# Streams of constant products on TensorE in the waits of a macaron transformer block

## The chip, the cores and the metric

The kernel runs on one core of one Trainium2 chip. The time is that of the device in microseconds (us): one launch, the median of three runs. The engines are PE (TensorE, matrix products; PEld is its weight load), DVE (VectorE), ACT (ScalarE), POOL (GpSimd) and SP (SyncE, which here issues most DMAs). PE's clock has two levels, 2.4 GHz and 1.2 GHz; the profile shows the granted one as 1.00 and 0.50, and a mean in between where a stretch has both.

## The reference

Three layers in a row over 2048 tokens of width 128, everything in f32. Cut to what matters:

```python
x = x + 0.5 * ffn(layernorm(x))          # layer 0
x = x + attention(layernorm(x))          # layer 1: 16 heads of 8, causal, 2048 keys
x = x + 0.5 * ffn(layernorm(x))          # layer 2, as layer 0

def ffn(x):                              # itself attention and then a mixture of experts
    h = rmsnorm(x, ln1_w)
    x = x + softmax(causal(rope(h @ wq) @ rope(h @ wk).T / sqrt(8))) @ (h @ wv) @ wo
    h = rmsnorm(x, ln2_w)
    probs = softmax(h @ router_w)                        # 8 experts
    topv, topi = top_k(probs, 2); topv /= topv.sum()
    weights = one_hot(topi) @ topv
    moe = sum over experts of (silu(h @ w_gate[e]) * (h @ w_up[e]) * weights[e]) @ w_down[e]
    return x + moe
```

Every expert has 448 hidden units. Only the two experts chosen for a token are computed.

## The kernel before

One loop `Fori(0, 3)` runs over the layers; layers 0 and 2 take the router and expert blocks, layer 1 jumps over them. A layer has three blocks, and at the end of a block each engine drains and all five meet at a barrier.

*Block 1, projections and attention.* The tokens are normalised, turned (L764) and projected in four chunks of 512 (L773 for the four q and k products with 512 columns, L781 for v). The rotated q and k are split into three bf16 parts, written to DRAM and read back as operands `qa` and `ka` of 96 rows. Behind the projections PE waits on `terms_ready` and `values_ready`, and then, for the first attention product (L809), on those loads. Attention has 16 chunks (4 head groups by 4 query chunks) and two streams of work on PE: "fillers" in banks 4 to 6, above all the row maxima (L809 and mask L812, reduced by DVE at L598), and the main stream, scores (L855, banks 0 to 3), exponentials on ACT (L747), weighted values (L868, bank 7). The order of both is computed ahead by `core_schedule()`, a list of events with estimated times; the change does not touch it. At the end of a chunk ACT copies the output (L754), PE turns it (L823, event "normalise") and DVE divides (L623, L624). When a query chunk is done in the last head group, PE turns it once more (L832, "turn"), DVE adds the bias (L632), and PE projects it (L840, "project"); DVE adds the residual and sums squares (L638 to L658). The last query chunk does this with nothing else left to do on PE.

*Block 2, the router.* DVE makes 16 normed tiles (L932), PE turns them (L885) and multiplies them with the router's 8 columns (L890, 16 f32 products of 8 columns, two records each in a trace). A chain of small DVE operations (L943 to L960) chooses the two experts per token. PE counts with two products (L896, L897); a second chain on DVE (L968 to L1026) makes the places of the tokens in expert slots and the one-hot tiles `moves` and `places`; PE multiplies these in 32 f32 products of 78 columns (L902), whose result DVE turns into the row numbers for the gathers (L1031 to L1034).

*Block 3, the experts.* POOL gathers 39 slots of 128 tokens by indirect DMA (L1053); PE turns a slot (L1103), multiplies with gate and up weights (L1118), turns the activation (L1127) and multiplies with the down weights (L1136). ACT and DVE work in between.

Bank 0 is written in block 1 by the first turns and by scores, in block 3 by the gate products; between these nobody reads it. `ones` is a 128 by 128 f32 tile of ones made once at the start and used as the left factor of L897.

Of the kernel before, what the change touches and what calls it, by code (L numbers as in the profile page):

```python
# [17 lines left out]
NC = T // CH  # L18
# [147 lines left out]
def macaron_kernel(nc, x_in, w5, b4, vecs, wo_w, rope, router, w_gate, w_up, w_down, out):  # L166
# [48 lines left out]
    ones = sb("ones", [128, 128])  # L215
# [132 lines left out]
    chunks, events, _ = core_schedule()  # L348
# [39 lines left out]
    def key_guard(b):  # L388

        return ka[64:96, b, :, :].rearrange("p h t -> p (h t)").bitcast(F32)  # L390


    with nc.Block() as block:

# [65 lines left out]
    with nc.Fori(0, NLAYER) as layer:  # L460

        with nc.Block() as block:
# [294 lines left out]
            def _(pe):  # L757
# [26 lines left out]

                pe.wait_ge(terms_ready, 4 * NC)
                pe.wait_ge(values_ready, NC)
                mi = 0
                pe.wait_ge(wo_loaded, 16)  # L790
                for ev in events:
# [6 lines left out]
                    if kind == "rowmax":  # L798
                        _, j, qt, h0, some, kc, final = ev
                        g, c = chunks[j]  # L800
                        b = g % 2
                        if qt == 0 and h0 == 0 and (kc == 0 or c == 0):
                            pe.wait_ge(group_loaded[g] if g else chunk_loaded[c], 16 * 6)
                        tile = TPC * c + qt
                        n = min(CH, (tile + 1) * 128 - kc * CH)
                        diag = kc == c
                        for k in range(some):
                            dst = ps[:, bank, k * n:(k + 1) * n]
                            ins = pe.matmul(dst, qa[0:KROWS, b, h0 + k, tile * 128:(tile + 1) * 128],  # L809
                                            ka[0:KROWS, b, h0 + k, kc * CH:kc * CH + n], start=True, stop=not diag)  # L810
                            if diag:
                                ins = pe.matmul(dst[:, n - 128:n], identb[:, :], mask_rows[:, :],  # L812
                                                start=False, stop=True)
                        ins.then_inc(filler_ready, 1)
                    elif kind == "maxout":
                        j = ev[1]
                        pe.wait_ge(maxima_ready, j + 1)
                        pe.transpose(ps[0:16, bank, 0:128], mx[:, j % MD, :], identf[:, :]).then_inc(filler_ready, 1)
                    elif kind == "normalise":
                        j = ev[1]  # L820
                        pe.wait_ge(output_copied, j + 1)
                        for k in range(TPC):
                            ins = pe.transpose(ps[:, bank, k * 128:(k + 1) * 128],  # L823
                                               otf[:, j % 2, k * 128:(k + 1) * 128], identf[:, :])
                        ins.then_inc(filler_ready, 1)
                        written = mi
                    elif kind == "turn":

                        c = ev[1]
                        pe.wait_ge(filler_used, written)  # L830
                        for k in range(TPC):
                            ins = pe.transpose(ps[:, bank, k * 128:(k + 1) * 128], onat[:, TPC * c + k, :], identf[:, :])  # L832
                        ins.then_inc(filler_ready, 1)
                        written = mi
                    elif kind == "project":
                        c = ev[1]
                        pe.wait_ge(filler_used, written)
                        for k in range(TPC):
                            t = TPC * c + k
                            ins = pe.matmul(ps[:, bank, k * 128:(k + 1) * 128], hT[:, t * 128:(t + 1) * 128],  # L840
                                            wos[:, 0:D], start=True, stop=True)
                        ins.then_inc(filler_ready, 1)
                    elif kind == "scores":
                        _, s, j, kt, h = ev
                        g, c = chunks[j]
                        b = g % 2
                        if kt == 0 and h == 0:
                            pe.wait_ge(guard_ready[j % MD], 16 * (j // MD + 1))
                        q0 = max(0, kt - TPC * c) * 128
                        n = CH - q0  # L850
                        u = HPG * s + h
                        if u >= SB:
                            pe.wait_ge(probs_ready, u - SB + 1)
                        dst = ps[:, u % SB, 0:n]
                        pe.matmul(dst, ka[0:KROWS, b, h, kt * 128:(kt + 1) * 128],  # L855
                                  qa[0:KROWS, b, h, c * CH + q0:(c + 1) * CH],
                                  start=True, stop=True).then_inc(scores_ready, 1)
                    elif kind == "values":
                        _, s, j, kt = ev
                        g, c = chunks[j]  # L860
                        q0 = max(0, kt - TPC * c) * 128
                        pe.wait_ge(probs_ready, HPG * (s + 1))
                        if kt >= TPC * c:
                            pe.wait_ge(masked, masks_to(j, kt))
                        if kt == 0 and j >= 1:
                            pe.wait_ge(output_copied, j)
                        for h in range(HPG):
                            ins = pe.matmul(ps[32 * h:32 * h + HD + 1, SB + MB, q0:CH],  # L868
                                            vv[:, kt, g * HPG + h, :], probs[:, s % 2, h, 0:CH - q0],
                                            start=kt == 0, stop=kt == TPC * (c + 1) - 1)  # L870
                        ins.then_inc(values_weighted, 1)


        with nc.Block() as block:

            @block.tensor
            def _(pe):
                with pe.If(layer != 1):
                    for c in range(NC):
                        if c >= 2:  # L880
                            pe.wait_ge(h2_copied, c - 1)
# [9 lines left out]
                                        start=True, stop=True)  # L891
                    ins.then_inc(logits_ready, 1)

                    pe.wait_ge(taken_ready, 1)
                    taken = gw[:, 5, :, :].rearrange("p t e -> p (t e)")
                    pe.matmul(ps[:, 7, 0:TT * E], below[:, :], taken, start=True, stop=True)  # L896
                    pe.matmul(ps[:, 7, TT * E:2 * TT * E], ones[:, :], taken, start=True, stop=True).then_inc(ranks_ready, 1)  # L897
                    pe.wait_ge(moves_ready, 1)
                    for q in range(NK // 8):
                        pe.wait_ge(places_ready, q + 1)  # L900
                        for k in range(8 * q, 8 * q + 8):
                            ins = pe.matmul(ps[:, 4, 0:2 * NSLOT], places[:, k, :],  # L902
                                            moves[:, k, :, :].rearrange("p s u -> p (s u)"),
                                            start=k == 0, stop=k == NK - 1)
                    ins.then_inc(slots_ready, 1)

            @block.scalar
            def _(act):
# [135 lines left out]
        with nc.Block() as block:  # L1044
# [53 lines left out]
            def _(pe):  # L1098
# [4 lines left out]
                    pe.transpose(ps[:, 7, 0:128], xring[:, u % XR, :], identf[:, :]).then_inc(tile_turned, 1)  # L1103

                with pe.If(layer != 1):
                    turn(0)
                    experts = []
                    for i in range(NSLOT + 2):
# [175 lines left out]
```

## Time and profile before

| | us |
|---|---|
| median of three runs | 1919.13 |
| lowest and highest run | 1913.59, 1921.05 |
| the profiled execution | 1916.23 |
| its span, first to last instruction | 1914.7 |
| PE busy | 1698.2 (89%) |
| DVE busy | 1369.8 (72%) |
| ACT busy | 1073.3 (56%) |
| mean granted clock of PE | 0.91 |

Times in the profile count from the start of the span. Layer 0 goes from there to about 709 us, layer 1 to 1221 us. A row of the timeline gives the start, the duration of the merged group, the engine, the line, what it writes and reads, its size and its count, and in brackets the idle time of the engine before it with what ended it. A busy PE is not PE at its peak: the same product at half the clock is busy for about twice the time. A record of PE includes the time until its last column is out, so products in a row are better priced from start to start.

### The profile page before, as it was taken

The page shows a single profiled execution, that of the slowest core. Times are in us where ns is not written, and L with a number is a line of the kernel's source. Part 1 is how long each engine was busy: PE and PEld are TensorE (multiplying, and loading weights), DVE is VectorE, ACT ScalarE, POOL GpSimd, SP SyncE. Part 2 cuts the span into 40 slices and gives each one's busy share as a digit, 9 for nine tenths or more (in the row PEclk, how much of TensorE's full clock was granted, in tenths as well). Part 3 has the DMA queues.
Part 4 walks back from the last instruction along what each step waited for, and adds up shares of the span by engine and source line. Part 5 has one row for each costly group of instructions (what it writes and reads, how often), then busy time and mean ns, then how long its engine had stood idle before and what let it go on. Part 6 is the DMA issues. An engine that isn't in the chain of part 4 may idle for free. (4 is left out here: it accounts for less than half of the span.)

```text
span 1914.7 us, 30151 instructions
## 1 busy us (share of the span) xinstructions
PE 1698.2 (89%) x10630; PEld 740.2 (39%) x10630; DVE 1369.8 (72%) x2705; ACT 1073.3 (56%) x2301; POOL 445.3 (23%) x491
## 2 busy tenths in 40 slices
PE   4899999999749947899999999579999999984895
PEld 2333333333247733233333342233333333324674
DVE  8788998986253338888999983388889998815333
ACT  3355777677604423356777678235576767771442
POOL 6300201111015647000102020260010100110564
PEclk9688999999859977889999999778899999995898
DMA  4500203300011135200202000242010020000113
GB/s 131 128 7 3 51 2 106 63 2 2 8 29 39 44 93 150 51 1 2 51 2 51 2 2 2 66 138 44 2 35 19 2 51 2 2 8 22 37 42 87
DMA packets 59432, 75.61 MB, mean 39 GB/s; under 512 B 9527, under 2 KB 52092, under 8 KB 57976
## 3 DMA queue, kind: packets, MB, share of 16 engines
q1 hardware_dynamic: 50056, 62.10, 12.6%
q0 software_dynamic: 4992, 9.32, 1.8%
q10 hardware_dynamic: 4224, 2.10, 0.4%
q8 instruction: 95, 1.56, 0.4%
q14 instruction: 65, 0.53, 0.1%
HBM read 52.97 MB, written 21.43 MB: 39 GB/s over the span
## 5 line engine op out<-in xcount | busy, mean ns | idle before, releaser
L747 ACT ACTIVATE probs<-ps 128x512 f32<-128x512 f32 (+3 forms) x1920 | 879.0, 543 | 471.7 <-PE ps L855 470.3
L598 DVE TENSOR_REDUCE mpart<-ps 128x1 f32<-128x512 f32 (+3 forms) x1680 | 1014.6, 665 | 115.9 <-PE ps L809 65.1
L809 PE MATMUL ps<-ka,qa 96*128 96x512 bf16 (+3 forms) x1920 | 670.3, 371 | 36.3 <-DMA ka<-ksplit 22.8
L855 PE MATMUL ps<-qa,ka 96*128 96x512 bf16 (+3 forms) x1920 | 617.0, 357 | 1.1 <-DMA qa<-guard 0.5
L868 PE MATMUL ps<-probs,vv 128*9 128x512 f32 (+3 forms) x3840 | 442.5, 533 | 8.8 <-ACT probs L747 8.1
L696 POOL TENSOR_SCALAR_AFFINE_SELECT probs<-probs 128x512 f32<-128x512 f32 x192 | 121.8, 634 | 1178.5 <-ACT probs L747 1178.5
L809 PEld LDWEIGHTS ps<-ka,qa 96*128 96x128 bf16 x1920 | 191.9, 101 | 480.2 <-DVE mpart L598 339.1
L855 PEld LDWEIGHTS ps<-qa,ka 96*128 96x128 bf16 x1920 | 183.7, 100 | 187.1 <-ACT probs L747 69.1
L812 PE MATMUL ps<-mask_rows,identb 128*128 128x128 bf16 x768 | 162.0, 236 | 0.0
L1189 DVE SCALAR_TENSOR_TENSOR probs<-probs,slot_w,ps 128x448 f32<-128x448 f32 x78 | 53.0, 680 | 120.0 <-PE ps L1118 120.0
L868 PEld LDWEIGHTS ps<-probs,vv 128*9 128x9 f32 x3840 | 57.8, 88 | 158.3 <-ACT probs L747 116.3
L1053 POOL DMA_INDIRECT arena<-tokens,from_row x78 | 76.8, 984 | 136.3 <-issue 79.8
L1063 POOL DMA_INDIRECT results<-hT,to_row x78 | 78.5, 1007 | 74.2 <-issue 42.1
L623 DVE RECIPROCAL rden<-ps 128x16 f32<-128x16 f32 x48 | 12.0, 250 | 113.3 <-PE ps L823 113.0
L812 PEld LDWEIGHTS ps<-mask_rows,identb 128*128 128x128 bf16 x768 | 80.4, 105 | 28.9 <-issue 2.2
L1136 PE MATMUL ps<-wds,probs 112*128 x624 | 82.8, 276 | 1.4 <-DVE hT L1196 1.2
L1147 ACT ACTIVATE hT<-ps 128x128 f32<-128x128 f32 x78 | 21.6, 277 | 110.3 <-PE ps L1103 110.3
L1136 PEld LDWEIGHTS ps<-wds,probs 112*128 112x128 f32 x624 | 75.8, 192 | 2.3 <-issue 2.3
L1118 PE MATMUL ps<-wgs,hT 128*128 x156 | 74.8, 562 | 0.8 <-ACT hT L1147 0.5
L1164 ACT ACTIVATE probs<-ps 112x512 f32<-112x512 f32 x78 | 46.6, 597 | 51.1 <-PE ps L1127 51.1
L1118 PE MATMUL ps<-wus,hT 128*128 x156 | 73.6, 555 | 0.0
L1158 ACT ACTIVATE probs<-ps 128x448 f32<-128x448 f32 x78 | 42.4, 543 | 39.4 <-PE ps L1118 39.2
(163 smaller groups left out, 1070.6 us busy)
## 6 DMA issues: line engine op xcount, KB each, us to landing
qa<-qsplit SPq DMA_DIRECT2D x27, 384.0 KB
ka<-ksplit SPq DMA_DIRECT2D x27, 384.0 KB
probs<-rope SPq DMA_DIRECT2D x12, 512.0 KB, 6.8
qa<-qsplit SPq DMA_DIRECT2D x36, 96.0 KB
ka<-ksplit SPq DMA_DIRECT2D x36, 96.0 KB
qsplit<-arena SPq DMA_DIRECT2D x6, 384.0 KB, 3.2
ksplit<-arena SPq DMA_DIRECT2D x6, 384.0 KB, 2.8
tokens<-arena SPq DMA_DIRECT2D x2, 1024.0 KB, 5.1
```

The lines of the kernel that those rows point to most:

```text
L598: dve.tensor_reduce(mpart[:, j % MD, h0:h0 + some, qt, kc], ps[:, bank, 0:some * w].rearrange("p (h w) -> p h w", h=some), axis=AX.X, op=A ...
L696: pool.affine_select(out=own, in_=own, compare_op=ALU.is_ge, fill=0.0, base=0, pattern=[[0, HPG], [1, 128]], channel_multiplier=-1).then_i ...
L747: act.activation(probs[:, s % 2, h, 0:n], ps[:, u % SB, 0:n], ACT.Exp, scale=SCALE).then_inc(probs_ready, 1)
L809: ins = pe.matmul(dst, qa[0:KROWS, b, h0 + k, tile * 128:(tile + 1) * 128], ka[0:KROWS, b, h0 + k, kc * CH:kc * CH + n], start=True, stop= ...
L812: ins = pe.matmul(dst[:, n - 128:n], identb[:, :], mask_rows[:, :], start=False, stop=True)
L855: pe.matmul(dst, ka[0:KROWS, b, h, kt * 128:(kt + 1) * 128], qa[0:KROWS, b, h, c * CH + q0:(c + 1) * CH], start=True, stop=True).then_inc( ...
L868: ins = pe.matmul(ps[32 * h:32 * h + HD + 1, SB + MB, q0:CH], vv[:, kt, g * HPG + h, :], probs[:, s % 2, h, 0:CH - q0], start=kt == 0, sto ...
L1053: pool.indirect_dma_start(xring[:, u % XR, :], None, tokens, bass.IndirectOffsetOnAxis(ap=from_row[:, u:u + 1], axis=0)).then_inc(tile_loa ...
L1063: pool.indirect_dma_start(results, bass.IndirectOffsetOnAxis(ap=to_row[:, u:u + 1], axis=0), obuf[:, u % OR, :], None, bounds_check=TOPK * ...
L1118: pe.matmul(ps[:, 2 * (i % 2) + k, 0:M], xt[:, i % 2, :], w[:, bass.ds(expert, 1), :].rearrange("p o m -> p (o m)"), start=True, stop=True ...
L1136: ins = pe.matmul(ps[:, 6, 0:D], atb[u % 2][:, k, :], wds[0:MR, bass.ds(experts[u], 1), k, :].rearrange("p o d -> p (o d)"), start=k == 0, ...
L1189: dve.scalar_tensor_tensor(acb[i % 2], sgb[i % 2], slot_w[:, i:i + 1], ps[:, 2 * (i % 2) + 1, 0:M], ALU.mult, ALU.mult).then_inc(act_ready, 1)
```

## The change

`spin(pe, n)` issues products of `ones` with itself, repeated over up to 512 columns, into bank 0: n is the number of 128-column pieces. Nobody reads the result and nothing waits for a semaphore of it, but PE works in order, so what stands behind a stream begins when the stream is through, and a block's end waits for it. Streams are added at eleven places; those of 26, 11 and the three of 2 run in all layers, the others in layers 0 and 2.

```diff
+    def spin(pe, n):
+        wide = ones[:, :].rearrange("p (o c) -> p o c", o=1)
+        for k in range(0, n, 4):
+            m = min(4, n - k)
+            pe.matmul(ps[:, 0, 0:m * 128].rearrange("p (o c) -> p o c", o=m), ones[:, :],
+                      wide.broadcast_to([128, m, 128]), start=True, stop=True)
...
+                spin(pe, 26)
                 pe.wait_ge(terms_ready, 4 * NC)
                 pe.wait_ge(values_ready, NC)
...
                     elif kind == "normalise":
                         j = ev[1]
+                        if j == len(chunks) - 1:
+                            spin(pe, 2)
                         pe.wait_ge(output_copied, j + 1)
...
                     elif kind == "turn":
                         c = ev[1]
+                        if c == NC - 1:
+                            spin(pe, 2)
                         pe.wait_ge(filler_used, written)
...
                     elif kind == "project":
                         c = ev[1]
+                        if c == NC - 1:
+                            spin(pe, 2)
                         pe.wait_ge(filler_used, written)
...
                         ins.then_inc(values_weighted, 1)
+                spin(pe, 11)
...
                 with pe.If(layer != 1):
+                    spin(pe, 8)
                     for c in range(NC):
...
                     ins.then_inc(logits_ready, 1)
+                    spin(pe, 22)
                     pe.wait_ge(taken_ready, 1)
...
                     pe.matmul(ps[:, 7, TT * E:2 * TT * E], ones[:, :], taken, start=True, stop=True).then_inc(ranks_ready, 1)
+                    spin(pe, 52)
                     pe.wait_ge(moves_ready, 1)
...
                     ins.then_inc(slots_ready, 1)
+                    spin(pe, 4)
...
                 with pe.If(layer != 1):
+                    spin(pe, 14)
                     turn(0)
```

From the end of attention to the first expert product, PE's program reads before, in the order in which PE takes it (the sizes are rows by columns of the output; the branches between the blocks are left out):

```order
L868 MATMUL ps<-probs,vv 9x128 x4
L823 MATMUL ps<-identf,otf 128x128 x4
L832 MATMUL ps<-identf,onat 128x128 x4
L840 MATMUL ps<-wos,hT 128x128 x4
...
L885 MATMUL ps<-identf,arena 128x128 x16
L890 MATMUL ps<-rts,hT 128x8 x16
L896 MATMUL ps<-rec,below 128x128
L897 MATMUL ps<-rec,ones 128x128
L902 MATMUL ps<-arena,probs 128x78 x32
...
L1103 MATMUL ps<-identf,arena 128x128 x2
```

Each of these rows from L823 on has a wait ahead of it, L890 and L897 excepted. In the changed kernel, whose own line numbers stand here, PE's program at the tail of attention reads (L833, L844 and L854 are L823, L832 and L840 of before):

```order
L882 MATMUL ps<-probs,vv 9x128 x4
L397 MATMUL ps<-ones 128x256
L833 MATMUL ps<-identf,otf 128x128 x4
L397 MATMUL ps<-ones 128x256
L844 MATMUL ps<-identf,onat 128x128 x4
L397 MATMUL ps<-ones 128x256
L854 MATMUL ps<-wos,hT 128x128 x4
L397 MATMUL ps<-ones 128x512 x2
L397 MATMUL ps<-ones 128x384
```

Three short streams stand ahead of the three waits, and the one of 11 closes the block. PE's program through the router and up to the first slot of the experts reads (L901 and L906 are L885 and L890 of before, L913, L914 and L920 are L896, L897 and L902):

```order
L397 MATMUL ps<-ones 128x512 x2
L901 MATMUL ps<-identf,arena 128x128 x16
L906 MATMUL ps<-rts,hT 128x8 x16
L397 MATMUL ps<-ones 128x512 x5
L397 MATMUL ps<-ones 128x256
L913 MATMUL ps<-rec,below 128x128
L914 MATMUL ps<-rec,ones 128x128
L397 MATMUL ps<-ones 128x512 x13
L920 MATMUL ps<-arena,probs 128x78 x32
L397 MATMUL ps<-ones 128x512
...
L397 MATMUL ps<-ones 128x512 x3
L397 MATMUL ps<-ones 128x256
```

Nothing changes places: the L397 rows are added between the old ones, ahead of the instruction that waits.

## Rows read from the trace of the kernel before

**Rows 1.** The page: parts 1 (busy, share) and 2 (PE's clock in 40 slices).

```profile
PE 1698.2 (89%) x10630; PEld 740.2 (39%) x10630; DVE 1369.8 (72%) x2705; ACT 1073.3 (56%) x2301; POOL 445.3 (23%) x491
...
PEclk9688999999859977889999999778899999995898
```

**Rows 2.** Waits of PE: us in total, times, longest.

```profile
PE ps L809 <- DMA ka<-ksplit: 22.8, 3, 7.8
```

**Rows 3.** Stretches: length, busy us (instructions) by engine, PE's clock, DMA share, GB/s.

```profile
45.00:49.00 4.00, 0.00 (x0) 0.00 (x0) 3.64 (x3) 2.44 (x5) 3.82 (x4) 0.53 0.79 205
49.00:55.00 6.00, 5.08 (x29) 2.92 (x30) 3.93 (x8) 1.74 (x2) 5.35 (x7) 0.50 0.81 243
...
58.00:69.00 11.00, 9.51 (x34) 3.71 (x33) 9.47 (x18) 2.52 (x5) 6.49 (x9) 0.54 0.46 115
...
168.00:512.00 344.00, 339.73 (x2357) 121.96 (x2355) 272.11 (x519) 250.62 (x550) 43.49 (x55) 1.00 0.13 32
```

**Rows 4.** Timeline, DVE: start, us, engine, line, what, [idle before, releaser].

```profile
51.07 6.13 DVE L598 TENSOR_REDUCE mpart<-ps 128x4 f32<-128x512 f32 x11 [2.28 <-PE ps L812]
...
517.20 0.69 DVE L638 TENSOR_TENSOR rec<-ps,vbc 128x512 f32<-128x512 f32 x1 [2.23 <-PE ps L840]
...
519.81 0.08 DVE L658 DVE_READ_ACCUMULATOR2_ANT rst<- 128x1 f32 x1
...
537.92 0.29 DVE L968 COPY rec<-ps 128x128 f32<-128x128 f32 x1 [0.64 <-PE ps L897]
```

**Rows 5.** Timeline, PE, L832 and L840 of two chunks.

```profile
481.71 0.66 PE L832 MATMUL ps<-identf,onat 128*128 128x128 f32 x4
...
484.14 1.16 PE L840 MATMUL ps<-wos,hT 128*128 128x128 f32 x8
...
513.09 1.09 PE L832 MATMUL ps<-identf,onat 128*128 128x128 f32 x4 [0.83 <-DVE onat L624]
...
515.12 2.05 PE L840 MATMUL ps<-wos,hT 128*128 128x128 f32 x8 [0.93 <-DVE hT L632]
```

**Rows 6.** Timeline, PE, the router and the first experts of layer 0.

```profile
522.68 4.27 PE L885 MATMUL ps<-identf,arena 128*128 128x128 f32 x16 [5.52 <-DVE arena L932]
526.79 4.00 PE L890 MATMUL ps<-rts,hT 128*128 128x8 f32 x32
536.66 0.79 PE L896 MATMUL ps<-rec,below 128*128 128x128 f32 x2 [5.87 <-DVE rec L960]
...
550.84 13.94 PE L902 MATMUL ps<-arena,probs 128*128 128x78 f32 x64 [12.96 <-DVE arena L1026]
570.18 0.47 PE L1103 MATMUL ps<-identf,arena 128*128 128x128 f32 x1 [5.41 <-DMA arena<-tokens,from_row]
...
572.35 1.86 PE L1118 MATMUL ps<-wgs,hT 128*128 x2 [0.49 <-ACT hT L1147]
```

**Rows 7.** Stretches of the tail, the router and the first experts.

```profile
508.00:512.00 4.00, 2.42 (x32) 0.96 (x24) 0.00 (x0) 2.12 (x8) 1.27 (x2) 1.00 0.00 0
...
526.00:529.00 3.00, 3.00 (x26) 2.82 (x25) 0.57 (x3) 2.48 (x3) 0.00 (x0) 0.92 0.47 136
...
528.00:530.00 2.00, 2.00 (x19) 2.00 (x19) 0.00 (x0) 0.89 (x1) 0.00 (x0) 0.98 1.01 289
...
552.00:564.00 12.00, 12.00 (x58) 12.00 (x57) 2.19 (x2) 0.00 (x0) 0.00 (x0) 0.50 0.00 0
...
576.00:578.00 2.00, 2.00 (x4) 0.86 (x4) 0.50 (x1) 0.77 (x2) 0.04 (x1) 0.58 0.13 33
```

**Rows 8.** Timeline, PE, products in a row during the projections.

```profile
26.72 1.06 PE L781 MATMUL ps<-otf,hT 128*128 128x128 f32 x8
27.66 3.70 PE L773 MATMUL ps<-hT,otf 128*128 128x512 f32 x8
31.20 0.60 PE L764 MATMUL ps<-identf,onat 128*128 128x128 f32 x4
```

**Rows 9.** Timeline, PE, the first wait for row maxima.

```profile
57.56 0.27 PE L818 MATMUL ps<-identf,mx 128*16 128x128 f32 x1 [1.63 <-DVE mx L605]
```

## The prediction

> **What bounds the kernel now.** I read the page's first two parts, then the granted clock in stretches, then PE's waits, then PE's timeline at the places where products are added. The reader is to see first that PE is busy 1698.2 us (89% of the span) and that its clock is not at full height everywhere: the line PEclk is at 10 tenths in the middle of each layer and at 5 to 8 at its edges [rows 1]. PE's clock has two levels here, 1.00 (2.4 GHz) and 0.50 (1.2 GHz). Between 168 and 512 us it stays at 1.00 with PE busy 339.7 of 344 us; there the change adds nothing [rows 3]. So the change can only win where PE works at 0.50 and something waits for it, and can only lose where a stream outlasts the wait in which it stands. Around PE's long waits I see four such places.
>
> 1. The start of attention. PE waits 7.8 us for ka [rows 2], the clock falls to 0.53 in that wait, and 49 to 55 us run at 0.50 [rows 3]. But VectorE reduces the row maxima there in one piece, 11 reductions in 6.13 us from 51.07 us on [rows 4]: it is the slower one, and PE waits for it right behind.
> 2. The tail of attention. L832 and L840 of the last chunk take 1.09 and 2.05 us at the low clock where the same lines took 0.66 and 1.16 us for another chunk at 481 to 485 us [rows 5].
> 3. The router (layers 0 and 2). DVE works a long chain of small operations; PE waits 5.87 us for `taken` and 12.96 us for `moves`, and then makes the 32 products of L902 (78 columns, two records each) in 13.94 us, all at 0.50, while DVE waits [rows 6, 7].
> 4. The first experts: from 572.35 us PE works without a gap, at 0.50 and, around 577 us, 0.58 [rows 6, 7]. From there to the end of the layer PE is what everybody waits for.
>
> **The price of a stream.** One f32 product of 512 columns: L773 begins at 27.66 and the line behind four of them at 31.20 us, 0.885 us each, or 0.221 us for 128 columns at 1.00 [rows 8]. At 0.50 the four L840 products of 128 columns take 2.05 us with their end [rows 5], so about 0.43 us for 128. The streams are then, high or low: 26 units 5.75 or 11.2 us; 2 units 0.44 or 0.9; 11: 2.4 or 4.7; 8: 1.8 or 3.4; 22: 4.9 or 9.5; 52: 11.5 or 22.4; 4: 0.9 or 1.7; 14: 3.1 or 6.0. What raises the clock shows at L885: 16 transposes begin at 522.68 us at 0.50, and at 526 to 529 us it is 0.92 [rows 6, 7]. A dense stream should do the same in a few us.
>
> The Trainium skill ("TensorE: Matmul & The Clock Gate", Part 4: PE-mode transpose) says that the full clock does not engage for PE's transposes. This trace disagrees, by those two rows: only transposes stand between 522.68 us and the rise. By the page L890 behind them would be slow before and after alike, and the term of L890 below would be nothing, 3.8 us less in the whole sum.
>
> **The change, part by part.** Of one router layer:
> - *Tail.* The streams of 2 stand in waits of 0.8 to 0.93 us [rows 5] and hide at either clock within 0.1 us. If they hold the clock, L832 and L840 return to 0.66 and 1.16 us: -1.3 us. If not, 0. I take -1.3, since the stretch before, 508 to 512 us, holds 1.00 with PE busy only 2.42 of 4 us [rows 7], and the streams only add to that.
> - *Streams of 11 and 8.* The 11 run beside DVE's last residual work: L840's consumer starts at 517.20 us and the last small operation of the block at 519.81 [rows 4], a cover of 2.6 us against 2.4 (or 4.7 at the low clock: up to +1.6). The 8 stand in the wait of L885 (5.52 us in all with what lies before). I take 0.
> - *L890.* A hazard that the change makes itself. Before, the clock rises just as L890 begins and falls at its end. Weight loads take 2.00/19 = 0.105 us at 0.98 and 12.00/57 = 0.21 us at 0.50 [rows 7], and L890 is 32 of them. After the change PE comes in at the high clock, the transposes (one per 0.27 us, half as dense as at low) and then 8-column products follow, and the clock should fall in L890 instead of rising before it. Ends 0 and +3.4; I take +1.9.
> - *Stream of 22.* It starts at the end of L890, then probably at 0.50, and rises on the way: 5 to 8 us against a wait of 5.87; L896 and L897 behind it fall from 1.26 us (536.66 to DVE's L968 at 537.92) to about 0.7 (4 records of 0.117 and their end) [rows 4, 6]. Ends -0.6 and +2.0; I take +0.7.
> - *Stream of 52.* 11.5 us at 1.00 in a wait of 12.96: hidden, 1.5 us of idleness left. (At 0.50 all through: +9.4, a rival below.)
> - *L902.* At the high clock the nearest row is L781, 8 records of 128 columns in 0.94 us from start to start [rows 8]: 64 x 0.117 = 7.5 us against 13.94. Ends 0 and -6.4. The remaining 1.5 us gap is the trouble: a wait of 1.63 us at 57 us was followed by 0.54 from 58 on [rows 3, 9]. L902 has more loading than streaming, and never got the clock up in 14 us. I take -4.0: the clock held for about two thirds of it.
> - *Stream of 4* lies beside the four small DVE operations that end the block; 0 or, low, +0.9: +0.3.
> - *Stream of 14 and first experts.* It stands in the 4 us between the block's start and the first gathered tile (570.18 us). All at 1.00, the 5.35 us from 572.35 shrink by half, -2.7; if it outlasts the tile, +0.9 comes back. I take -2.1.
>
> Sum of a router layer: -1.3 + 1.9 + 0.7 - 4.0 + 0.3 - 2.1 = -4.5 us, twice: -9.0. Layer 1 has the tail alone: -1.3 (DVE ends its block there too). The start of attention, three times: the stream of 26 is hidden (5.75 of 7.8 us, at 1.00 since the projections before it are), but DVE is behind PE; what is won is the first group of four, 0.85 us at low and half at high: -0.4, with ends +1.7 and -2 for cold stretches that move later in the layer. Three: -1.2. In all -11.5 us (-9.0, -1.3, -1.2). Against the execution's own 1916.23 us (span 1914.7 and 1.5 around it) this is 1904.7. The median of the three runs, 1919.13, stands 2.9 above that execution, so the forecast is 1907 to 1908; I say **1907**.
>
> **Rivals.**
> *A. Short gaps leave the clock alone.* L890 keeps its speed, L902 runs all at 1.00, the experts too: per router layer -1.3 - 0.6 - 6.4 - 2.7 = -11.0; with layer 1 and better starts -25 us: 1894. For it: 504 to 512 us stays at 1.00 in spite of waits of 0.8 us. Against: the fall behind 57 us. The Trainium skill (same page, "Why this matters for your kernels") has this rule, that only idle gaps longer than those left here throttle the engine; this trace speaks against it with the same fall.
> *B. The clock falls in the rest of the wait before L902.* The sum without the 4.0: -0.5 per router layer, -1.3, -1.2, in all -3.5 us: 1915.6. For it: L890 and L902 at 0.50 all through and the 57 us case. Against: only 1.5 of 13 us remain idle.
> *C. The streams run low and outlast their waits.* The point from which it decides is the clock at the end of L890. If the stream of 22 needs the whole low time (9.5 against 5.9 us, +3.6), a third of the 52 runs low too (7.7 and 7.5 against 12.96, +2.2), L890 takes its +3.4, and neither L902 nor the experts gain: +9.2 per router layer, 1919.1 + 18.4 = 1937.5. If constants do not raise the clock at all, the 52 alone add 9.4, beyond that. Against it: projections, transposes and experts each raised the clock while they ran. That is also the case in which the change doesn't do what it says.
>
> **How the numbers follow.** Forecast 0.42, A 0.15, B 0.35, C 0.08. The range: A's end (1894) to a little above B (1915.6 and what DVE-bound starts may cost), 1893 to 1920; C is left out. What can be told from no change is 0.5%, 9.6 us: below 1909.5 is faster. Faster: A and three quarters of the forecast's own spread, 0.49. Within 0.5%: B and the rest, 0.43. Slower: C, 0.08.
>
> **What would show it.** The clock in the stretch of L902 and its duration: 7.5 us (A), 9 to 11 (forecast), 13.9 (B). L890: 4.0 us or 5 to 7. L896's idle time: none if the 22 outlast the wait. L1118's first pair: 1.86 or 0.92 us. L840 at the tail: 1.16 or 2.05. PE's wait for `moves` is to shrink from 12.96 to about 1.5 us; if instead DVE's row L968 starts later relative to L943 than 7.1 us, the stream of 22 costs more than I said. The forecast is wrong if L902 gains nothing, or if attention in any layer, from its first L855 to its last L823, moves by more than 2 us.

## The result, and the profile after

| | before | after |
|---|---|---|
| median, run side by side (20 runs each) | 1917.32 | 1913.14 |
| lowest and highest run | 1913.59, 1923.58 | 1909.39, 1917.88 |
| the profiled execution | 1916.23 | 1914.05 |
| its span | 1914.7 | 1912.5 |
| mean granted clock of PE | 0.910 | 0.938 |

The ratio of the times is 0.9975, with a 95% interval of 0.9967 to 0.9982. The kernel became 4.2 us faster, where the prediction summed 11.5 us. It is a real gain, smaller than the 0.5% that the prediction took as its bound, and inside its range; but the size is off by a factor of 2.7, and one term of the sum carries most of that.

The page of the kernel after, parts 1 and 2 (busy time; PE's clock in 40 slices), answers to [rows 1]:

```profile
PE 1767.2 (92%) x10812; PEld 764.4 (40%) x10812; DVE 1370.8 (72%) x2705; ACT 1073.0 (56%) x2301; POOL 445.0 (23%) x491
...
PEclk9789999999979978889999999887999999998998
```

PE is busy 69 us longer and has 182 more instructions, all of them streams, and the clock is higher in the slices at the ends of attention. DVE has as much to do as before.

PE's timeline of layer 0 from the tail of attention to the first experts (start, us, engine, line, what, and in brackets the idle time before it with its releaser). L833, L844, L854 are L823, L832, L840 of before; L901, L906, L913, L914, L920 are L885, L890, L896, L897, L902; L1122 and L1138 are L1103 and L1118. It answers to [rows 5, 6]:

```profile
515.10 0.66 PE L844 MATMUL ps<-identf,onat 128*128 128x128 f32 x4 [0.31 <-DVE onat L631]
515.59 0.60 PE L397 MATMUL ps<-ones 128*128 128x256 f32 x2
516.59 1.16 PE L854 MATMUL ps<-wos,hT 128*128 128x128 f32 x8 [0.41 <-DVE hT L639]
517.59 2.53 PE L397 MATMUL ps<-ones 128*128 128x512 f32 x6
521.18 1.98 PE L397 MATMUL ps<-ones 128*128 128x512 f32 x4 [1.07 <-PEq L469]
523.27 4.27 PE L901 MATMUL ps<-identf,arena 128*128 128x128 f32 x16
527.38 5.60 PE L906 MATMUL ps<-rts,hT 128*128 128x8 f32 x32
532.84 8.02 PE L397 MATMUL ps<-ones 128*128 128x512 f32 x12
540.69 0.38 PE L913 MATMUL ps<-rec,below 128*128 128x128 f32 x2
540.91 0.39 PE L914 MATMUL ps<-rec,ones 128*128 128x128 f32 x2
541.14 11.32 PE L397 MATMUL ps<-ones 128*128 128x512 f32 x26
554.26 12.34 PE L920 MATMUL ps<-arena,probs 128*128 128x78 f32 x64 [1.80 <-DVE arena L1045]
566.40 2.00 PE L397 MATMUL ps<-ones 128*128 128x512 f32 x2
568.86 5.37 PE L397 MATMUL ps<-ones 128*128 128x512 f32 x8 [0.47 <-PEq L889]
574.06 0.27 PE L1122 MATMUL ps<-identf,arena 128*128 128x128 f32 x1
...
575.78 1.01 PE L1138 MATMUL ps<-wgs,hT 128*128 x2 [0.69 <-ACT hT L1167]
```

And the stretches of the kernel after (length, busy us by PE, PEld, DVE, ACT, POOL, then the clock, DMA share, GB/s), to set beside [rows 7]:

```profile
523.00:527.00 4.00, 3.84 (x16) 1.98 (x15) 4.00 (x16) 1.66 (x3) 0.00 (x0) 1.00 0.00 0
528.00:533.00 5.00, 5.00 (x29) 5.00 (x29) 0.00 (x0) 1.46 (x2) 0.00 (x0) 0.57 0.75 212
541.00:552.00 11.00, 11.00 (x29) 4.90 (x27) 9.87 (x32) 0.00 (x0) 0.00 (x0) 1.00 0.00 1
554.00:556.00 2.00, 1.74 (x15) 1.74 (x16) 2.00 (x3) 0.00 (x0) 0.00 (x0) 1.00 0.00 0
556.00:566.00 10.00, 10.00 (x50) 10.00 (x49) 1.62 (x2) 0.00 (x0) 0.00 (x0) 0.50 0.00 0
569.00:573.00 4.00, 4.00 (x5) 1.69 (x6) 2.27 (x4) 0.00 (x0) 2.91 (x3) 0.50 0.06 16
576.00:578.00 2.00, 2.00 (x7) 1.02 (x7) 0.33 (x1) 1.52 (x3) 1.39 (x3) 1.00 0.20 39
```

Read the two together. The tail is short again. The transposes now run at 1.00, and behind them the clock falls inside L906 (0.57), so the stream of 22 starts low: 8.02 us, where 22 x 0.221 would be 4.9. The stream of 52 stands at 1.00 all through, but 1.80 us are left behind it. L920 starts high and is low from 556 us on, 1.8 us behind its start (1.3 us in layer 2): some 15 of its 64 records lie in the 2 us at 1.00, and the rest in the 10 us at 0.50. It hands a low clock to the streams of 4 and 14, and that of 14 (5.37 us) holds back the first slot. Only then is the clock up.

Segments between the starts of instructions, in us (of a router layer, layer 0 and layer 2; the names are those of before):

| from, to | before | after | predicted change |
|---|---|---|---|
| last L823, last L840 (also layer 1) | 4.75, 4.75 | 3.40, 3.40 | -1.3 |
| last L840, first L885 | 5.94, 5.94 | 5.80, 5.80 | 0 |
| L890, L943 | 4.04, 4.03 | 5.64, 4.44 | +1.9 |
| L943, L968 | 7.09, 7.09 | 8.32, 7.87 | +0.7 |
| L902, L1031 | 13.98, 13.98 | 12.38, 12.78 | **-4.0** |
| L1031, first L1103 | 5.37, 4.61 | 7.42, 7.00 | +0.3, with the row below -1.8 in all |
| first L1103, last L1136 | 120.71, 121.28 | 117.64, 117.51 | |
| last L823, last L1136 | 178.91, 178.72 | 177.62, 175.82 | -4.5 |

### The profile page after: what moved, and what is told of

Same layout as the page of the kernel before. It is cut to its first block and busy times, and to the rows that moved or that the text cites. A ratio compares the mean times of both kernels' runs of the same rounds, so it can differ in the third digit from the quotient of the medians.

```text
span 1912.5 us, 30506 instructions
## 1 busy us (share of the span) xinstructions
PE 1767.2 (92%) x10812; PEld 764.4 (40%) x10812; DVE 1370.8 (72%) x2705; ACT 1073.0 (56%) x2301; POOL 445.0 (23%) x491
## 5 line engine op out<-in xcount | busy, mean ns | idle before, releaser
L820 PE MATMUL ps<-mask_rows,identb 128*128 128x128 bf16 x768 | 157.8, 231 | 0.0
L1209 DVE SCALAR_TENSOR_TENSOR probs<-probs,slot_w,ps 128x448 f32<-128x448 f32 x78 | 53.1, 680 | 115.9 <-PE ps L1138 115.9
L397 PE MATMUL ps<-ones 128*128 128x512 f32 (+2 forms) x182 | 87.0, 624 | 3.1 <-PEq L469 2.1
L1138 PE MATMUL ps<-wgs,hT 128*128 x156 | 71.6, 541 | 1.2 <-ACT hT L1167 1.2
L1138 PE MATMUL ps<-wus,hT 128*128 x156 | 71.4, 539 | 0.0
```

The lines of the kernel that those rows point to most:

```text
L397: pe.matmul(ps[:, 0, 0:m * 128].rearrange("p (o c) -> p o c", o=m), ones[:, :], wide.broadcast_to([128, m, 128]), start=True, stop=True)
L1138: pe.matmul(ps[:, 2 * (i % 2) + k, 0:M], xt[:, i % 2, :], w[:, bass.ds(expert, 1), :].rearrange("p o m -> p (o m)"), start=True, stop=True ...
```

## The experiments

Two theories of the missing gain were on record before them. *The wait* (first theory): the 1.8 us of idleness that the stream of 52 leaves before L902 make the clock fall in it. *Too thin* (second theory): L902, which loads weights longer than it streams, cannot hold the high clock whatever stands before it. For L890's loss the suspicion was the streams of 11 and 8, which bring PE in high so that it falls in L890. Runs e1 to e4 are compared with one set of runs of the kernel before, e5 to e8 with a second, both on one chip on which the kernel before takes 1933.73 and 1935.49 us; e9 to e12 with a third, on another chip where it takes 1919.32. In brackets behind a ratio stands its 95% interval. Lengths of stretches go from the start of one PE or DVE instruction to the start of another.

**e1: the stream of 52 made 58**, six pieces (1.3 us) longer. This and the next diffs are against the changed kernel.

```diff
-                    spin(pe, 52)
+                    spin(pe, 58)
```

> The changed kernel with the stream of 52 made 58, so that it reaches almost up to L920 (L902 of before): the wait of 1.80 us ahead of it should shrink to about 0.5 us. Theory 1 (the wait makes the clock fall): L920 then runs at 1.00, about 7.5 us instead of 12.3 and 12.7, and the kernel gains 9 to 10 us against the changed one, about 1904. Theory 2 (L920 itself is too thin to hold the clock, whatever stands ahead): it starts at 1.00, falls within some 3 to 4 us all the same, lasts 10 to 11 us, and the kernel gains 3 to 4 us.

Measured: 1919.98 us against 1933.73, ratio 0.9924 (0.9911 to 0.9938). L902 to L1031 took 7.41 us in both layers. PE's timeline and a stretch of e1:

```profile
534.34 12.61 PE L397 MATMUL ps<-ones 128*128 128x512 f32 x30
547.46 7.37 PE L920 MATMUL ps<-arena,probs 128*128 128x78 f32 x64 [0.51 <-DVE arena L1045]
```

```profile
547.00:555.00 8.00, 7.54 (x65) 7.45 (x66) 3.95 (x6) 0.00 (x0) 0.00 (x0) 1.00 0.01 2
```

The same 64 records, as thin as before, stay at 1.00 throughout with PEld busy 7.45 of 8 us. *Too thin* falls; *the wait* stands. The price of 7.5 us that the prediction worked out for the high clock [rows 8] was right. The longer stream does two things at once, though: it shortens the wait and adds 1.3 us of dense products ahead of it, and no run separates the two; "the wait" stands for both here. By the ratios e1 is 12 us faster than the changed kernel on the same chip (e5), more than the 9 to 10 us of the first theory: the first slot is no longer held up either (5.34 and 4.64 us from L1031 to L1103, against 7.38 and 7.36 in e5).

**e2: without the streams of 11 and 8.**

```diff
-                spin(pe, 11)
...
-                    spin(pe, 8)
```

> The changed kernel without the streams of 11 and 8. Theory 1 (they bring PE to the router's transposes at the high clock, which then falls in the 8-column products): the transposes begin at 0.50, the clock rises in them or right behind, L906 (L890 of before) lasts 4.0 us again instead of 5.60 and 4.41, and the stream of 22 starts at or near 1.00 and ends before DVE has the sets: 1.0 to 2.8 us less per router layer up to L968, 2 to 4 us in all. Theory 2 (the loss there is chance): L906 lasts as in the changed kernel and the whole is within 1 us of it.

Measured: 1933.63 us, ratio 0.9992 (0.9983 to 1.0001). L890 became slower, not faster: 6.87 us in both layers to DVE's L943. PE's timeline and stretches of e2:

```profile
519.32 4.42 PE L901 MATMUL ps<-identf,arena 128*128 128x128 f32 x16 [5.52 <-DVE arena L951]
523.54 6.84 PE L906 MATMUL ps<-rts,hT 128*128 128x8 f32 x32
```

```profile
519.00:524.00 5.00, 4.68 (x19) 3.46 (x20) 4.21 (x16) 2.01 (x4) 0.00 (x0) 0.50 0.00 0
524.00:530.00 6.00, 6.00 (x29) 6.00 (x30) 0.00 (x0) 1.66 (x2) 0.00 (x0) 0.50 0.62 178
```

The first theory was wrong, and so is the notion that the two streams cause the loss at L890. Without the streams the clock is at 0.50 from the transposes to the end of L890. The same 16 transposes raised it in the kernel before [rows 6, 7] and did not here: with the tail at the high clock and 5.52 us of waiting behind it, the rise before L890 did not come. Every layer of the kernel before, e4 and e12, which all have the tail at the low clock, shows 4.00 to 4.04 us there, and both layers of e2 6.87; why the same transposes raise the clock in the one case and not in the other is open. A sum should not have taken the rise as given.

**e3: without the streams of 4 and 14.**

```diff
-                    spin(pe, 4)
...
-                    spin(pe, 14)
```

> The changed kernel without the streams of 4 and 14. From L1031 (slot weights copied) to the last down product of the layer it took 126.0 us before and 125.1 and 124.5 us after the change. Theory 1 (they win 2.7 us at the first experts and give half of it back by holding up the barrier and the first slot's turn): this kernel is 1 to 1.5 us slower per router layer than the changed one, 2 to 3 in all. Theory 2 (they give back all of it): within 0.5 us.

Measured: 1928.22 us, ratio 0.9960 (0.9945 to 0.9974), better than the whole change (e5 below). L1031 to the first L1103 is 5.34 and 4.69 us again, 2.0 and 2.7 less than with the streams at the low clock, and the experts from L1118 to the last L1136 take 126.33 and 125.00 us against e5's 125.48 and 125.83. Neither theory held: the first had expected e3 to be slower, the second equal. e3 begins its experts at 0.50 and e5 at 1.00, and over the two layers they take the same time: on this chip, where that stretch scatters by over 2 us from kernel to kernel (125.0 to 127.8), a warm start can't be seen.

**e4: the stream of 26 alone**, all others taken out.

> The kernel before with the stream of 26 behind the projections alone, in three layers. My prediction's term: -1.2 us in all, with attention starting at the high clock. Rival: since DVE sets the pace there, the clock falls a few us later instead, the gain is nothing, and the stretch from the first maxima product to the last turn of attention stays 462, 459 and 459 us within the scatter of 1 to 2 us that comes from where the clock happens to fall.

Measured: 1933.90 us, ratio 0.9992 (0.9980 to 1.0004): not to be told from nothing. The other segments came back to those of before: tail 4.75, L890 4.03, L902 to L1031 13.98 in both layers.

**e5: the changed kernel again**, with these.

> The changed kernel again, on the chip of these runs, to compare the others with on one chip. Where the experts take 126 us in every kernel (as in the four runs before, against 116 to 119 us in the two first profiles), its gain at the first experts, 2.7 us per router layer, should be lost and only the cost of the streams of 4 and 14 be left: ratio to the kernel before 0.998 to 1.000 instead of 0.9975.

Measured: 1934.06 us against 1935.49, ratio 0.9988 (0.9977 to 1.0000). Its router is that of the first profile (L902 to L1031 12.41 and 12.44; L1031 to L1103 7.38 and 7.36), with L890 at 5.69 and 5.72. But from L1118 to the last L1136 it takes 125.48 us where the first profile has 115.92 (layer 0). The waits of layer 0 between 600 and 680 us (us in total, times, longest), and that stretch, of e5:

```profile
ACT probs L1184 <- remote: 27.0, 9, 3.2
DVE probs L1209 <- PE ps L1138: 21.8, 13, 2.0
POOL results L1082 <- DVE hT L1216: 18.2, 8, 2.4
DVE hT L1216 <- remote: 17.4, 8, 2.3
```

```profile
600.00:680.00 80.00, 76.07 (x414) 52.52 (x413) 23.32 (x48) 31.76 (x73) 48.28 (x49) 1.00 0.14 39
```

In the first profile of the kernel after, the same stretch reads:

```profile
600.00:680.00 80.00, 80.00 (x463) 58.33 (x463) 26.43 (x55) 38.33 (x82) 53.26 (x54) 1.00 0.17 44
```

On the one chip PE is what everybody waits for (80.00 of 80 us); on the other each engine does about a tenth less in the same 80 us, with waits whose releaser the profile does not show. It was so in every kernel on that chip (experts of 125 to 128 us in all eight, e4 without any stream in the router among them), so it is no effect of the change, and it hides the gain of warm first experts there. What slows that chip is open.

**e6: 58, without 4 and 14.**

```diff
-                    spin(pe, 52)
+                    spin(pe, 58)
...
-                    spin(pe, 4)
...
-                    spin(pe, 14)
```

> 58 in place of 52, and no streams of 4 and 14. Theory (the two parts are independent): it has the 5 us per router layer of the 58 and, where the experts aren't held up by PE, 0.5 to 2 us more per router layer than with the streams of 4 and 14; about 0.989 to 0.992. Rival (L920 leaves the clock high, and the streams of 4 and 14 cost nothing at the high clock, as in the run with 58, where the first slot's turn came 5.34 us behind the copy of the slot weights, as early as before): within 1 us of the run with 58 alone, 0.9924.

Measured: 1926.84 us against 1935.49, ratio 0.9950 (0.9937 to 0.9963), against e1's 0.9924. L902 to L1031 is 7.41 again. Behind a high L902 the streams of 4 and 14 cost nothing (e1: L1031 to L1103 5.34 and 4.64 with them, 5.22 and 4.71 without), and the experts took 127.63 and 127.75 us here against 126.0 in both layers of e1. Neither expectation held: e6 is neither faster than e1 nor within 1 us of it, but 5 us slower by the ratios. A warm start is not the reason, since the first experts begin at 0.50 in both (562.5 to 565.8 us in e1, 565.0 to 568.6 us in e6); 1.6 to 1.7 us per layer lie within the scatter of that stretch on this chip, and what made the rest is open. In e3 the same edit won; in e6 it lost. Up to the first slot the two streams are harmless where the clock is handed to them high, and a delay of 0.7 to 2.7 us where it is low (e2, e5, e7).

**e7: without the three streams of 2.**

> The changed kernel without its three streams of 2 at the tail of attention. Theory (they alone keep the clock up there): last turn to last project product takes 4.75 us again instead of 3.40, in all three layers, 4 us in all, if the rest stays. Rival: the 1.35 us come back in what follows, since L906 (the 8-column products) meets the change of the clock at another moment: L906 back at 4.0 us, and the total within 1 us of the changed kernel.

Measured: 1937.85 us, ratio 1.0005 (0.9994 to 1.0016). PE's timeline of e7:

```profile
517.02 2.04 PE L854 MATMUL ps<-wos,hT 128*128 128x128 f32 x8 [0.94 <-DVE hT L639]
518.85 3.89 PE L397 MATMUL ps<-ones 128*128 128x512 f32 x6
```

The tail is at 4.75 us in all three layers, so the streams of 2 are worth 1.35 us each time. In layers 0 and 2 it also takes 6.67 us instead of 5.80 from L840 to L885: the stream of 11 starts low, needs 3.89 us, and now outlasts DVE's last residual work. That is the hazard which the prediction priced at up to +1.6 and set at nothing; the streams of 2 are what keeps it away. Up to L1031 the parts add up to 3.7 us: 3 x 1.35 + 2 x 0.87 for the lost streams, 2 x 0.6 for a slower L902, less 2 x 1.0 for L890 and 2 x 0.65 for the stream of 22 behind it. From L1031 to the last L1136 e7 takes 1.0 and 0.4 us more than e5. By the ratios e7 stands 3.3 us worse than e5 (0.0017 of 1935); the two intervals, each 4 us wide, overlap, so the segments show this loss and the totals alone do not. The theory held; the rival saw something true, since L890 came back to 4.69 us, but not enough of it.

**e8: 58, without 4 and 14, and the router's turns filled.** A bf16 product of the identity with itself stands behind each of the 16 transposes.

```diff
                             ins = pe.transpose(ps[:, 4 + c % 2, k * 128:(k + 1) * 128], h2[:, t, :], identf[:, :])
+                            pe.matmul(ps[:, 0, 0:128], identb[:, :], identb[:, :], start=True, stop=True)
```

> As the run with 58 and without 4 and 14, and a bf16 product of 128 columns (identity by identity, into bank 0) behind each of the 16 turns of the router. Theory (the thin pace of the turns at the high clock and then of the 8-column products makes the clock fall in them): the clock stays high into the 8-column products, which last 4.0 to 5 us instead of 5.6 to 5.7, and the stream of 22 ends in time: 1 to 2 us less per router layer. Rival (the 8-column products alone let it fall): no change, or up to 1 us more, since each turn has another product ahead.

Measured: 1920.75 us against 1935.49, ratio 0.9922 (0.9907 to 0.9936); e6, which differs by the filling alone, has 0.9950. L890 to L943 falls to 3.73 us, L943 to L968 to 6.97, in both layers. That is more than the 1 to 2 us per router layer that were expected: 3.2 us in these two segments, 2.7 by the ratios. The clock now stays high to the end of L890, so the 8-column products alone do not let it fall; the cause of L890's loss in the changed kernel is the sparse turns at the high clock.

**e9: all streams, 58, the turns filled.**

> All streams of the changed kernel, 58 in place of 52, and a bf16 product behind each of the 16 turns of the router. The runs so far give the parts: L920 7.4 us, the 8-column products 3.7 us, the first experts 1.7 us shorter than without the streams of 4 and 14, at no cost since they run at the high clock. It should be the fastest of all: about 3 us under the run with 58 alone and 3 us under the one that filled the turns without 4 and 14, a ratio of 0.990 to 0.991. Rival: the scatter of where the clock falls in attention (3 us per layer) swallows it.

Measured: 1897.50 us (6 runs, 1893.63 to 1904.34) against 1919.32, ratio 0.9890 (0.9872 to 0.9909). PE's timeline and stretches of e9 (its lines behind the turns are one higher):

```profile
522.72 3.69 PE L907 MATMUL ps<-rts,hT 128*128 128x8 f32 x32
526.26 6.67 PE L397 MATMUL ps<-ones 128*128 128x512 f32 x12
...
546.33 7.37 PE L921 MATMUL ps<-arena,probs 128*128 128x78 f32 x64 [0.50 <-DVE arena L1046]
553.53 1.07 PE L397 MATMUL ps<-ones 128*128 128x512 f32 x2
555.17 3.26 PE L397 MATMUL ps<-ones 128*128 128x512 f32 x8 [0.58 <-PEq L889]
559.08 0.33 PE L1123 MATMUL ps<-identf,arena 128*128 128x128 f32 x1 [0.65 <-DMA arena<-tokens,from_row]
560.37 0.33 PE L1123 MATMUL ps<-identf,arena 128*128 128x128 f32 x1 [0.96 <-DMA arena<-tokens,from_row]
561.34 1.73 PE L1139 MATMUL ps<-wgs,hT 128*128 x2 [0.64 <-ACT hT L1168]
```

```profile
518.00:522.00 4.00, 3.88 (x29) 2.08 (x28) 3.96 (x16) 1.38 (x3) 0.00 (x0) 1.00 0.00 0
522.00:526.00 4.00, 4.00 (x38) 3.78 (x36) 0.44 (x2) 2.29 (x3) 0.00 (x0) 1.00 0.64 181
526.00:533.00 7.00, 7.00 (x19) 3.43 (x19) 5.49 (x21) 0.31 (x1) 0.00 (x0) 0.76 0.17 49
546.00:553.00 7.00, 6.67 (x60) 6.68 (x60) 3.67 (x4) 0.00 (x0) 0.00 (x0) 1.00 0.01 2
561.00:565.00 4.00, 3.67 (x6) 1.84 (x7) 0.31 (x1) 2.03 (x4) 3.05 (x4) 0.57 0.19 49
```

L890 is high to its end; the clock falls only behind it, in the stream of 22 (0.76), where there is slack for it. L902 stays high, the stream of 14 takes 3.26 us and waits for the first slot instead of holding it back (0.65 us for the DMA). But the first experts are not warm: the stream of 14 ends at 558.4 us, PE makes two single turns in the 2.9 us behind it, and the first pair of L1139 (L1118 of before) takes 1.73 us, not 1.01 as in the changed kernel, with the clock at 0.57 from 561 to 565 us. The "1.7 us shorter" first experts of the expectation did not come (125.21 and 124.86 us from L1031 to the last L1136, against 125.39 and 125.15 in e12 below, which has neither stream). This is the best version measured.

**e10: e9 without the stream of 26.**

> The same without the stream of 26 at the start of attention. Theory (it wins nothing, since DVE sets the pace there and the clock falls a little later anyway): the same time within 2 us. Prediction's term: 1.2 us slower. Attention from the first maxima product to the last turn stays 458 to 462 us in each layer either way.

Measured: 1903.67 us, ratio 0.9912 (0.9897 to 0.9928). The medians are 6.2 us apart, more than the 2 us that were expected, but the interval meets that of e9. From the first L809 to the last L823, 33 layers of eleven profiles with the stream of 26 take 460.2 us in the mean and 9 layers of three without it 461.2, with an error of about 0.5 on the difference. In e10 this stretch takes 461.8, 461.9 and 462.2 us, in e9 459.2, 459.1 and 462.1; single layers lie between 457.9 and 463.1 in all fourteen profiles. The term may be -1 us per layer, or nothing.

**e11: 55**, half way between 52 and 58.

> The changed kernel with 55 in place of 52: the wait ahead of L920 becomes about 1.2 us, between the 1.8 us after which the clock fell in L920 and the 0.5 us after which it held. Theory 1 (any short wait will do as long as most of the time around it is dense): L920 takes 7.4 us as with 58, ratio 0.993. Rival: 1.2 us is too long as well, and L920 takes 10 to 12.4 us, at least in one of the two layers.

Measured: 1907.04 us, ratio 0.9927 (0.9905 to 0.9948). PE's timeline of e11:

```profile
538.62 11.97 PE L397 MATMUL ps<-ones 128*128 128x512 f32 x28
551.74 7.37 PE L920 MATMUL ps<-arena,probs 128*128 128x78 f32 x64 [1.15 <-DVE arena L1045]
```

1.15 us of waiting leave the clock high in both layers (L902 to L1031 7.41 and 7.41); 1.80 us did not, in any of the ten router layers that had it (the first profile, e2, e3, e5, e7: 12.4 to 13.0 us). Nothing between 1.15 and 1.80 us was tried.

**e12: the kernel before with the stream of 22 and one of 58 alone.**

> The kernel before with only two streams, 22 and 58, in the router. Theory (the parts are independent): the stream of 22 starts low and delays L968 by up to 1 us, the 58 starts high or nearly so, L920 takes 7.4 us; 5 to 6 us less per router layer, ratio 0.994 to 0.995. Rival: the 58 start partly low, last over 13 us, and L920 starts 1 to 3 us late: ratio 0.996 to 0.998.

Measured: 1906.40 us, ratio 0.9934 (0.9921 to 0.9947). Two streams of eleven places bring more than the whole change does (0.9975) and over half of what e9 does: L902 to L1031 7.41 us in both layers. L890 is at 4.00 and 4.03 as before, and L943 to L968 is 8.32 and 8.29, 1.2 us more than before: the stream of 22 starts low and outlasts DVE's chain. Its first experts begin low too. PE's timeline and a stretch of e12:

```profile
568.23 1.85 PE L1138 MATMUL ps<-wgs,hT 128*128 x2 [0.49 <-ACT hT L1167]
```

```profile
568.00:572.00 4.00, 3.77 (x6) 1.94 (x7) 0.30 (x1) 2.05 (x4) 2.98 (x4) 0.50 0.20 49
```

## Why the prediction was right in its sign and wrong in its size

**The step that failed** is the term "L902: I take -4.0: the clock held for about two thirds of it". It measured -1.6 and -1.2 us; over two layers 5.2 us of the missing 7.3. The prediction had all that it needed: a price of 7.5 us at the high clock, which all seven profiles with a high L902 confirm (7.41), the rest of the wait (1.5 us, in truth 1.8), and a row with a wait of 1.63 us and a fall behind it [rows 3, 9]. It then split the difference between the two ends. No run showed such a middle: either the product stays high (waits of 0.5 and 1.15 us, -6.6 us), or the clock falls 1 to 2 us into it (wait of 1.8 us, -1.0 to -1.6). That is close to rival B, and nearer to it than to the forecast in size: B's sum was -3.5 us, the forecast's -11.5, the runs gave -4.2. B was not exact either, since the clock did not fall in the wait but just behind it. The row that argued for B should have weighed more than the argument that only 1.5 of 13 us remain idle.

**The stream of 22** was given +0.7 and cost +1.2 and +0.8. It starts at 0.50 and takes 8.02 us (7.57 in layer 2) against the 5 to 8 that were named; L896 had no idle time left, as the prediction said it would show. The mechanism was right, the value too small.

**L890** was given +1.9 and cost +1.6 and +0.4 (+1.7 in e5). The size was about right, the cause only half. The clock does fall inside it when PE comes in high behind the transposes, as the prediction said; but e2 shows that it is worse when PE comes in low behind a high tail (6.87 us): the rise that the prediction read from [rows 6, 7] is not to be had from 16 transposes in every case. What decides is that the clock is high when L890 begins and that the turns before it are dense enough to keep it so (e8, e9: 3.73).

**The end of the router and the first experts** were given -1.8 in all (streams of 4 and 14, first experts) and brought -1.0 and -1.4 (126.08 and 125.88 us from L1031 to the last L1136 before, 125.06 and 124.51 after). The first pair of L1118 took 1.01 us, high as predicted. The stream of 14 was costed at the high clock with +0.9 for a miss; handed the low clock by L902 it took 5.37 us and delayed the first slot by 2.0 and 2.4 us, which warm experts paid back. This is the second consequence of the failed step. The other half of the term was right: from the first L1118 to the last L1136 the kernel before takes 118.55 and 118.76 us, the kernel after 115.92 and 115.99, which is the -2.7 of the sum within 0.1 us. No run has both the first slot on time and warm first experts. e9 and e12 have the slot on time and begin the experts low, and take 117.61 and 117.70, and 117.83 and 118.04 us, for this stretch. If 115.9 us could be had with the slot on time, that would be worth an estimated 1.7 us per router layer beyond e9 (117.6 less 115.9); no run shows it.

**The tail** was given -1.3 per layer and brought -1.35 in all three, with 0.66 and 1.16 us for L844 and L854, to the hundredth the rows of the chunk at 481 us [rows 5]. e7 adds 0.9 us per router layer that the sum did not credit.

**The start of attention** was given -0.4 per layer. e4 (0.9992, 0.9980 to 1.0004) and e10 leave it between nothing and -1 us. From a layer's first turn to its last L823 the profile after shows 495.3, 491.7 and 489.7 us, the one before 493.2, 490.2 and 490.6: 2.8 us more in all. With the same streams e5 has 491.7, 489.3 and 490.2. The prediction's own sign of being wrong, more than 2 us between a layer's first L855 and last L823, did not show: that stretch moved by -1.55, +0.29 and -0.99 us. A single profile cannot carry a term of this size; and scatter of this kind is about what stands between the 2.2 us by which the profiled executions differ and the 4.2 of the medians.

**Rival A** is half alive. Its rule, that short gaps leave the clock alone, holds ahead of L902 at 0.5 and 1.15 us and fails at 1.80. The Trainium skill ("TensorE: Matmul & The Clock Gate", "Why this matters for your kernels") warns only of longer gaps than this. The rows of the kernel after disagree with it as a rule for this place: with 1.80 us ahead of 64 thin products the clock read 0.50 for the remaining 10 us. **Rival C** did not happen: the streams of 52 ran at 1.00 in every profile that has them.

**The chances** were added up a little wrong: A's 0.15 and three quarters of the forecast's 0.42 are 0.465 and not 0.49 for "faster", and B with the rest 0.455 and not 0.43. Nothing else hangs on it.

## What to carry to other kernels

A stream of dummy products does not earn anything where it stands, only by the clock that it hands to the next real work; so measure it by that work, and bring it close to the end of the wait: here six more pieces (1.3 us) of 52 turned a ratio of 0.9988 into 0.9924 on one chip. Where a term depends on which of two levels the clock has, price both ends, look for the row that decides, and say which: here the value between them was the one that no run showed. A stream that starts low takes longer, here 8.02 us against 6.67 (22 pieces), 3.89 against 2.53 (11) and 5.37 against 3.26 (14), so put one only where the wait covers its low length, or behind work that keeps the clock up. And look at the clock in the work behind each stream even in the best version: in e9 the stream of 14 ends 2.9 us ahead of the first experts, and they begin low.

## What the runs showed of the hardware that was not expected

- A wait of 1.15 us before L902 left the clock at 1.00 for 7.4 us of thin products, one of 1.80 us let it fall 1 to 2 us into them, in ten of ten router layers.
- Products of 78 columns, with PEld busy all the time, held a high clock for 7.4 us (e1, e6, e8 to e12) but never raised a low one in 10 to 14 us (before; after, 556 to 566 us).
- 16 f32 transposes raised the clock in the kernel before [rows 6, 7] and left it at 0.50 in e2. A bf16 product behind each of them costs 0.05 us in the whole segment (4.16 against 4.11 us) and keeps the clock high into L890.
- From the first L1118 to the last L1136 the kernels take 118 us on one chip (e9 to e12) and 125 to 128 us on another (e1 to e8), with a granted clock of 1.00 from 600 to 680 us on both (e9, e5); the cause is not in the profile.
- In every kernel whose L902 ran high, the clock was at 0.50 for 3.4 to 4.3 us at the start of the first experts, with or without the streams of 4 and 14.
